# A fused four-layer cross-attention kernel: transposes of the row maxima with 128 weight columns instead of 4

## The chip, the cores and the metric

The kernel runs on one core of one Trainium2 chip. The metric is the device time of one execution in microseconds (us), median of the runs shown; lower is better. Five engines matter: TensorE (PE, with its weight loads as PEld), VectorE (DVE), ScalarE (ACT), GpSimd (POOL) and the DMA queue that SyncE feeds (SPq).

## The reference

The input `x` (4 batches, 1024 tokens, 256 channels) goes through four cross-attention layers over the same context `ctx_2048` (4 batches, 154 keys, 512 channels). Layers 0 and 2 are wide (16 heads of 64), with a bias on the logits of chosen keys; layers 1 and 3 are narrow (16 query heads of 16 on 4 key heads) with an RMS norm ahead.

```python
# wide (L0, L2)
q = (x @ Wq) ; k = (ctx @ Wk) ; v = (ctx @ Wv)             # 16 heads of 64
logits = einsum('bhqd,bhkd->bhqk', q, k) * 64 ** -0.5
logits = logits + col_bias                                  # -20 * (1 - mask) on 4 chosen keys
x = einsum('bhqk,bhkd->bhqd', softmax(logits), v) @ Wo + bo + x
# narrow (L1, L3)
xn = x * rsqrt(mean(x * x) + 1e-5) * norm_w
scores = einsum('btgrd,bsgd->bgrts', xn @ wq, ctx @ wk) / 16 ** 0.5
x = x + einsum('bgrts,bsgd->btgrd', softmax(scores), ctx @ wv) @ wo
```

The softmax subtracts the maximum of each row of logits over the 154 keys; the kernel finds these maxima first and folds them, with a minus sign, into the score matmuls.

## The kernel before, in words

`prepare` makes the keys, the values and split weights (the first 190 us). `layers` then runs two layers at a time over 4 batches and 2 pairs of layers, in halves of 512 tokens. Its work is cut into steps: 16 to a batch, each of four heads on one half of the tokens, 128 in all. A step has these parts:

- "query": six fp32r matmuls of 512 columns each (L1470) make the queries of two heads or of a group; ACT copies them (L1225, L1226), and DVE rounds and subtracts (L1377 to L1380). Only then can "max" of that step start.
- "max", eight per step: a rough bf16 product of 128 tokens with the 154 keys of two heads (L1485 wide, L1489 narrow) in a PSUM bank of `general`, which DVE reduces to two maxima per token (L1390), so that `tops` gets 4 maxima for each of 4 blocks of 128 tokens.
- "turn": four transposes (L1496) bring these maxima from columns into rows. The block of `tops` is the weight operand and the identity `ident_bf` (128 columns) streams past it; ACT copies the 4 rows, negated, into rows of `q_aux` (L1248).
- "rest" and "score": the real products (L1513, L1516, L1524, L1525) and ACT's exponentials (L1238); "value": products with the values and the sums (L1540 with 64 weight columns, L1544, L1550 and L1554 with 32; in narrow steps L1560 and L1566 with 32). "sums", "inverse", "scale", "norm", "low" and "output" (L1584, six matmuls for each of two banks) finish a chunk.

All engines walk one hand-written list (`FIRST`, `ORDER`, `LAST`, joined in `PLAN`), so every engine issues its share of the parts in that order and waits by semaphores. The part "turn n" stands in it mostly behind the query of a later step and ahead of a "value", a "rest" or a "max". Of the 128 turns, counted along PE's order of instructions, the neighbours are:

| before the turn | after the turn | turns |
|---|---|---|
| 128 weight columns | 128 weight columns | 64 |
| 128 weight columns | 64 weight columns (L1540) | 47 |
| 64 weight columns (L1540) | 64 weight columns (L1540) | 9 |
| 128 weight columns | 32 weight columns (L1560) | 5 |
| 64 weight columns | 128 weight columns | 2 |
| 32 weight columns | 128 weight columns | 1 |

Of the 67 turns with 128 weight columns behind them, 47 have an fp32 or fp32r matmul there (23 L1524, 20 L1470, 4 others) and 20 a bf16 one (19 L1489, 1 L1485).

The rows of zeros and constants that several tiles need are cleared by DVE and POOL when `layers` starts; SyncE waits for six of DVE's memsets (`rows_cleared`, L1179) before it goes on issuing loads.

Of the kernel before, what the change touches and what calls it, by code (L numbers as in the profile page):

```python
# [16 lines left out]
BF16 = mybir.dt.bfloat16  # L17
# [5 lines left out]
P = 128  # L23
# [477 lines left out]
def first_tile(n):  # L501

    return 12 * (n // 8) + (2 * (n % 8) if wide(n) else 4 + n % 8)
# [318 lines left out]
def layers(nc, ins, dr, out):  # L822

    ctx = ExitStack()
    with ctx:
        def sb(name, shape, dt=F32):
            return ctx.enter_context(nc.sbuf_tensor(name, shape, dt))
# [17 lines left out]
        w_aux, n_aux = (sb(a + "_aux", [P, H, P], BF16) for a in "wn")  # L845
        w_top, n_top = (sb(a + "_top", [P, H, KEYS], BF16) for a in "wn")
        w_rest, w_aux_rest = sb("w_rest", [P, H, 32]), sb("w_aux_rest", [P, H, 32], BF16)
        n_pair_rest, n_aux_rest = sb("n_pair_rest", [P, KVN, P], F32R), sb("n_aux_rest", [P, KVN, P], BF16)
# [5 lines left out]
        q_aux = sb("q_aux", [P, 2, 2, 4, TOK], BF16)  # L854
# [4 lines left out]
        spread_sums, inv = sb("spread_sums", [P, TOK // 8]), sb("inv", [P, TOK // 8])  # L859
        inv_b, inv_n = sb("inv_b", [P, 2, TOK]), sb("inv_n", [P, 2, TOK])  # L860
        a_hi, a_lo = sb("a_hi", [P, 2, TOK], F32R), sb("a_lo", [P, 2, TOK], F32R)
        tops = sb("tops", [P, 2, 4, 4], BF16)
        meansq, rate, power = sb("meansq", [P, 4]), sb("rate", [P, 4]), sb("power", [P, 4])
        ident, ident_bf, ones = sb("ident", [P, P]), sb("ident_bf", [P, P], BF16), sb("ones", [P, 1])
        sel, sel_rest = sb("sel", [P, 4, 32]), sb("sel_rest", [P, 4, 32])
# [3 lines left out]
        out_ps = ctx.enter_context(nc.psum_tensor("out_ps", [P, 2, 512], F32))  # L869
        sum_ps = ctx.enter_context(nc.psum_tensor("sum_ps", [P, 512], F32))  # L870

        ROWS_CLEARED, CLEARED = 6, 9


        WIDE_QUERY, KEY_ROWS, WIDE_OUT = 16 * 2, 16 * 8, 16 * 2
# [479 lines left out]

        @block.vector
        def _(dve):
            for buf in (w_top, q_aux, w_aux, w_aux_rest, n_aux, n_aux_rest):
                nc.vector.memset(buf[:].bitcast(F32), 0.0).then_inc(rows_cleared, 1)
            for buf in (n_top, n_val_rest, sel, sel_rest):  # L1360
                nc.vector.memset(buf[:].bitcast(F32), 0.0).then_inc(cleared, 1)
# [3 lines left out]
            for g in range(4):  # L1365
                nc.vector.memset(sel[:, g, 8 * g:8 * g + 8], 1.0)
                for j in range(4):
                    last = nc.vector.memset(sel_rest[32 * j:32 * j + REST, g, 8 * g:8 * g + 8], 1.0)
# [73 lines left out]
        def _(pe):  # L1442
# [3 lines left out]
            def bank(use):  # L1446

                if USE[use] >= GB:
                    w, what, n, k, m = GENERAL[USE[use] - GB]
                    read = reader[what]  # L1450
                    wait(pe, read.sem, read.after(w, what, n, k) - (read.times - 1 - m if what == "output" else 0))
                return general[:, USE[use] % GB, :]

            def do(it, what, n, k):
                if what == "query":
# [9 lines left out]
                    ps = bank((it, what, n, k, 0))  # L1465
# [3 lines left out]
                    for i, (l, r) in enumerate(pairs):  # L1469
                        last = nc.tensor.matmul(ps, l, r, start=(i == 0), stop=(i == len(pairs) - 1))  # L1470
                    last.then_inc(pe_query.sem, 1)
                elif what == "max":
# [7 lines left out]
                    ps = bank((it, what, n, k, 0))  # L1480
                    sub, pair = slice(k % 4 * P, k % 4 * P + P), k // 4
                    q = q_aux[:, half_of(n), slot(n)]
                    if wide(n):
                        for i in range(2):
                            last = nc.tensor.matmul(ps[:, i * KEYS:(i + 1) * KEYS], q[:, 2 * pair + i, sub],  # L1485
                                                    w_top[:, 4 * (n % 4) + 2 * pair + i, :], start=True, stop=True)
                    else:
                        h = 4 * (n % 4) + 2 * pair
                        last = nc.tensor.matmul(ps[:, 0:2 * KEYS], q[:, n % 2, sub],  # L1489
                                                n_top[:, h:h + 2, :].rearrange("p h k -> p (h k)"), start=True, stop=True)  # L1490
                    last.then_inc(pe_max.sem, 1)
                elif what == "turn":
                    wait(pe, dve_max.sem, dve_max.after(it, "max", n, 7))
                    ps = bank((it, what, n, k, 0))
                    for sub in range(4):
                        last = nc.tensor.transpose(ps[0:4].bitcast(BF16)[:, sub * P:(sub + 1) * P], tops[:, n % 2, sub, :], ident_bf[:])  # L1496
                    last.then_inc(pe_turn.sem, 1)
                elif what in ("rest", "score"):
                    number = pe_score.after(it, what, n, k)
                    ps = score_ps[:, number % 2, :]  # L1500
# [10 lines left out]
                    if what == "rest" and wide(n):  # L1511
# [3 lines left out]
                        for j in range(4):  # L1515
                            last = nc.tensor.matmul(ps[32 * j:32 * j + 32], w_aux_rest[:, 4 * g + j], q_aux[:, t, s, j, :],  # L1516
                                                    start=False, stop=True, skip_group_check=True)
                    else:
# [6 lines left out]
                        last = nc.tensor.matmul(ps, keys[1], q_aux[:, t, s, unit, :], start=False, stop=True)  # L1525
                    last.then_inc(pe_score.sem, 1)
                elif what == "value":
# [9 lines left out]
                    if wide(n):  # L1537
                        for i in range(2):
                            h = 4 * g + 2 * k + i
                            last = nc.tensor.matmul(out_ps[64 * i:64 * i + 64, k, :], w_val[:, h * DW:(h + 1) * DW], probs[:, 2 * k + i, :],  # L1540
                                                    start=True, stop=False, skip_group_check=True)
                        if k == 1:
# [9 lines left out]
                            for j in range(4):  # L1552
                                rows = slice(32 * j, 32 * j + REST)
                                last = nc.tensor.matmul(sum_ps[SUMS[j]], sel_rest[rows, g, :], rest[rows],  # L1554
                                                        start=False, stop=(g == 3), skip_group_check=True)
                    else:
                        out = out_ps[:, tile % 2, :]
                        for j in range(4):
                            at = 32 * block_of(n, j)
                            last = nc.tensor.matmul(out[at:at + 32], n_val[:, g, :], probs[:, j, :],  # L1560
                                                    start=True, stop=False, skip_group_check=True)
                        if n % 2:
                            for step in (n - 1, n):
                                for j in range(4):
                                    rows, at = slice(32 * j, 32 * j + REST), 32 * block_of(step, j)
                                    last = nc.tensor.matmul(out_ps[at:at + 32, first_tile(step) % 2, :], n_val_rest[rows, step % 4, :],  # L1566
                                                            probs_rest[rows, step % 4, :], start=False, stop=True, skip_group_check=True)
                    last.then_inc(pe_value.sem, 1)
                elif what == "output":
# [8 lines left out]
                    for m in range(KC):  # L1578
                        ps = bank((it, what, n, k, m))
# [3 lines left out]
                        for i, (l, r) in enumerate(pairs):  # L1583
                            last = nc.tensor.matmul(ps, l, r, start=(i == 0), stop=(i == len(pairs) - 1))  # L1584
                        last.then_inc(pe_output.sem, 1)
                elif what == "give":
# [5 lines left out]
                    ps = bank((it, what, n, k, 0))  # L1592
                    of = fetch_to[:, i % 2] if n < 6 else x[:, n % 2]
                    for t in range(2):
                        for c in range(KC):
                            at = (2 * k + t) * P
                            last = nc.tensor.transpose(ps[:, t * C + c * P:t * C + c * P + P], of[:, c, at:at + P], ident[:])
                    last.then_inc(pe_give.sem, 1)
                elif what == "square":
                    wait(pe, act_square.sem, act_square.after(it, "squares", n, k))  # L1600
                    ps = bank((it, what, n, k, 0))
                    for sub in range(4):
                        for c in range(KC):
                            last = nc.tensor.matmul(ps[:, sub:sub + 1], xn[:, c, sub * P:(sub + 1) * P], ones[:],
                                                    start=(c == 0), stop=(c == KC - 1))
                    last.then_inc(pe_square.sem, 1)
                elif what == "rate":
                    wait(pe, pool_rate.sem, pool_rate.after(it, "square", n, k))
                    ps = bank((it, what, n, k, 0))
                    for sub in range(4):  # L1610
                        last = nc.tensor.transpose(ps[:, sub * P:(sub + 1) * P], rate[:, sub:sub + 1].to_broadcast([P, P]), ident[:])
                    last.then_inc(pe_rate.sem, 1)

            def query_for(n, k):

                return ("query", n, k) if wide(n) else ("query", n - n % 2, 0)

            each_batch(pe, do)


# [5 lines left out]
def store_outputs(nc, dr, out):  # L1626

    layers(nc, dr["ins"], dr, out)
# [32 lines left out]
```

## Time and profile before

| | |
|---|---|
| median of 3 runs | 1791.41 us (1787.99 to 1791.44) |
| the profiled execution's own time | 1801.82 us |
| its span, first to last instruction | 1800.0 us |
| mean granted TensorE clock | 0.963 of 2.4 GHz |
| PE busy | 1655.3 us (92%), 10732 matmuls |
| DVE busy | 1221.1 us (68%) |
| ACT busy | 1024.6 us (57%) |
| POOL busy | 462.0 us (26%) |

PE's busy time counts the modelled tail of each matmul, so matmuls that are issued back to back overlap in it; how fast PE goes is read from the distance between two starts in the timeline. A row of the timeline that holds several matmuls (x4) gives the start of the first and the time until the end of the last.

### The profile page before, as it was taken

To read this page: it belongs to the slowest core of one execution; us is meant where nothing else is said; L and a number is where in the kernel's file an instruction comes from. 1 tells how busy PE (TensorE), PEld (TensorE's weight loads), DVE (VectorE), ACT (ScalarE), POOL (GpSimd) and SP (SyncE) were. 2 spreads that over 40 slices of the span, in tenths; PEclk is the share of its full clock that TensorE was granted. 3 is DMA by queue.
4 is the path that set the end of the run, shared out by engine and by line. 5 is a ranking of instruction groups with operands and counts; after the bars stand their busy time and mean duration, and the time that the engine had idled before them with its cause. 6 is when DMAs were issued, how large, how long until landed. Compare 5 with 4: busy or idle time off the path is not lost.

```text
span 1800.0 us, 29688 instructions
## 1 busy us (share of the span) xinstructions
PE 1655.3 (92%) x10732; PEld 894.5 (50%) x10732; DVE 1221.1 (68%) x2339; ACT 1024.6 (57%) x1737; POOL 462.0 (26%) x325
## 2 busy tenths in 40 slices
PE   6999568999999999999999999999999999999884
PEld 5787334444544445454545454545444545444442
DVE  4474536676868786777766777677777877786551
ACT  2120146576666676667666766576666766666442
POOL 4242301122222232213231313122322222232212
PEclk9998689999999999999999999999999999999987
DMA  8996621050215121513244222413251225031422
GB/s 279 326 315 207 178 80 38 27 103 25 75 38 116 33 72 29 127 24 82 66 106 105 62 62 78 88 40 71 47 111 26 80 40 121 26 78 23 119 67 79
DMA packets 177459, 165.30 MB, mean 92 GB/s; under 512 B 91802, under 2 KB 133146, under 8 KB 175778
## 3 DMA queue, kind: packets, MB, share of 16 engines
q1 hardware_dynamic: 175010, 152.91, 33.2%
q10 hardware_dynamic: 2304, 10.49, 1.5%
q8 instruction: 87, 1.43, 0.3%
q14 instruction: 58, 0.48, 0.1%
HBM read 117.73 MB, written 45.58 MB: 91 GB/s over the span
## 4 chain that ended last, share of the span: by engine, by line
PE 48%; issue 12%; DVE 11%; SPq 6%; POOL 5%; ACT 3%; DMA 3%; POOLq 0%; ACTq 0%; DVEq 0%
PE general L1584 9%; PE general L1470 8%; PE score_ps L1524 6%; PE score_ps L1525 5%; PE out_ps L1540 4%; POOL kept L1346 4%; PE general L1489 3%; PE general L1485 3%; SPq L1022 3%; DVE q_aux L1378 2%; PE score_ps L1513 2%; PE out_ps L1560 2%; DVE q_pair L1379 2%; DVE q_pair L1380 2%; DVE q_aux L1377 2%
## 5 line engine op out<-in xcount | busy, mean ns | idle before, releaser
L1390 DVE TENSOR_REDUCE tops<-general 128x2 bf16<-128x308 f32 x1024 | 434.9, 471 | 125.7 <-PE general L1485 75.2
L1238 ACT ACTIVATE probs<-score_ps 128x512 f32<-128x512 f32 x512 | 299.1, 598 | 171.8 <-PE score_ps L1525 160.0
L1346 POOL TENSOR_TENSOR kept<-kept,inv_b 128x512 f32<-128x512 f32 x128 | 169.0, 1341 | 470.7 <-DMA inv_b<-scratch_inverses 458.5
L1377 DVE CAST q_aux<-q_pair 64x512 bf16<-64x512 f32 x160 | 89.1, 557 | 194.9 <-ACT q_pair L1226 193.6
L1248 ACT ACTIVATE q_aux<-general 4x512 bf16<-4x512 bf16 x320 | 187.2, 585 | 40.2 <-PE general L1496 34.5
L1225 ACT ACTIVATE q_pair<-general 64x512 fp32r<-64x512 f32 x160 | 94.5, 591 | 128.7 <-PE general L1470 127.4
L1334 POOL TENSOR_TENSOR x_lo<-xn,x_hi 128x1024 fp32r<-128x1024 f32 x32 | 75.8, 2370 | 322.6 <-ACT x_hi L1206 188.8
L1485 PE MATMUL general<-w_top,q_aux 128*128 128x154 bf16 x1024 | 131.9, 235 | 26.8 <-DVE q_pair L1380 17.2
L1403 DVE TENSOR_TENSOR a_lo<-kept,a_hi 128x512 fp32r<-128x512 f32 x160 | 121.4, 791 | 44.8 <-ACT a_hi L1285 44.0
L1423 DVE TENSOR_TENSOR x<-general,x 128x512 f32<-128x512 f32 x160 | 106.9, 689 | 62.9 <-PE general L1584 61.8
L1285 ACT ACTIVATE a_hi<-kept 128x512 fp32r<-128x512 f32 x160 | 93.5, 625 | 97.6 <-PE general L1584 43.1
L1260 ACT ACTIVATE kept<-out_ps 128x512 f32<-128x512 f32 x192 | 104.2, 595 | 70.6 <-PE sum_ps L1554 55.2
L1489 PE MATMUL general<-n_top,q_aux 128*128 128x308 bf16 x512 | 126.4, 302 | 17.4 <-DVE q_pair L1380 13.3
L1485 PEld LDWEIGHTS general<-w_top,q_aux 128*128 128x128 bf16 x1024 | 79.8, 99 | 119.4 <-issue 56.6
L1524 PE MATMUL score_ps<-q_pair,w_pair 128*128 128x512 f32 x256 | 124.4, 490 | 14.4 <-ACT probs_rest L1238 14.2
L1540 PE MATMUL out_ps<-probs,w_val 128*64 128x512 f32 x512 | 135.7, 615 | 0.0
L1524 PE MATMUL score_ps<-q_pair,n_pair 128*128 128x512 f32 x256 | 126.4, 505 | 4.4 <-ACT probs L1238 4.4
L1346 POOL TENSOR_TENSOR kept<-kept,inv_n 128x512 f32<-128x512 f32 x64 | 82.4, 1308 | 185.9 <-DMA inv_n<-scratch_inverses 185.9
L1470 PE MATMUL general<-x_hi,wq_hi 128*128 128x512 f32 x256 | 114.7, 448 | 13.9 <-POOL x_lo L1334 12.5
L1584 PE MATMUL general<-a_hi,wo_hi 128*128 128x512 f32 x256 | 112.3, 439 | 5.6 <-DVE q_pair L1380 2.8
L1379 DVE TENSOR_TENSOR q_pair<-general,q_pair 64x512 fp32r<-64x512 f32 x160 | 109.5, 684 | 5.0
L1380 DVE TENSOR_TENSOR q_pair<-general,q_pair 64x512 fp32r<-64x512 f32 x160 | 111.0, 694 | 2.2
(149 smaller groups left out, 3238.7 us busy)
## 6 DMA issues: line engine op xcount, KB each, us to landing
inv_b<-scratch_inverses SPq DMA_DIRECT2D x128, 256.0 KB, 4.8
xn<-scratch_stream SPq DMA_DIRECT2D x16, 512.0 KB, 3.4
w_pair<-scratch_wk_hi SPq DMA_DIRECT2D x32, 256.0 KB
x<-scratch_stream SPq DMA_DIRECT2D x16, 512.0 KB, 3.3
inv_n<-scratch_inverses SPq DMA_DIRECT2D x256, 32.0 KB, 1.8
scratch_stream<-x SPq DMA_DIRECT2D x14, 512.0 KB, 4.8
scratch_wk_hi<-p_kout_hi SPq DMA_DIRECT2D x16, 308.0 KB
p_raw<-in_L_xattn_Wk_dram SPq DMA_DIRECT2D x4, 1024.0 KB, 7.9
```

What stands on the lines that cost most here:

```text
L1238: nc.scalar.activation(dst, score_ps[:, number % 2, :], ACT.Exp, scale=scale).then_inc(act_exp.sem, 1)
L1248: last = nc.scalar.activation(q_aux[a:a + 4, half_of(n), slot(n), j, :], ps[0:4].bitcast(BF16)[:, 0:TOK], ACT.Copy, scale=-1.0)
L1346: last = nc.gpsimd.tensor_tensor(tiles[i], tiles[i], (inv_b, inv_n)[n % 2][:, i, :], ALU.mult)
L1379: nc.vector.tensor_tensor(q_pair[64:P, s, j, :], ps[0:64], q_pair[0:64, s, j, :], ALU.subtract)
L1380: last = nc.vector.tensor_tensor(q_pair[0:64, s, j + 1, :], ps[64:P], q_pair[64:P, s, j + 1, :], ALU.subtract)
L1390: last = nc.vector.tensor_reduce(tops[:, n % 2, sub, 2 * pair:2 * pair + 2], src, AX_X, ALU.max)
L1470: last = nc.tensor.matmul(ps, l, r, start=(i == 0), stop=(i == len(pairs) - 1))
L1485: last = nc.tensor.matmul(ps[:, i * KEYS:(i + 1) * KEYS], q[:, 2 * pair + i, sub], w_top[:, 4 * (n % 4) + 2 * pair + i, :], start=True, st ...
L1489: last = nc.tensor.matmul(ps[:, 0:2 * KEYS], q[:, n % 2, sub], n_top[:, h:h + 2, :].rearrange("p h k -> p (h k)"), start=True, stop=True)
L1524: nc.tensor.matmul(ps, keys[0], q_pair[:, s, unit, :], start=True, stop=False)
L1540: last = nc.tensor.matmul(out_ps[64 * i:64 * i + 64, k, :], w_val[:, h * DW:(h + 1) * DW], probs[:, 2 * k + i, :], start=True, stop=False, ...
L1584: last = nc.tensor.matmul(ps, l, r, start=(i == 0), stop=(i == len(pairs) - 1))
```

## The change

`tops` gets 128 columns for each block of 128 tokens instead of 4. DVE clears it once at the start; the maxima are still written to columns 0 to 3, and the other 124 stay zero. The four transposes of a turn now take the whole block as weights and write 128 rows of the bank instead of 4; ACT still reads rows 0 to 3. The count of memsets that `rows_cleared` stands for goes from 6 to 7.

```diff
-        tops = sb("tops", [P, 2, 4, 4], BF16)
+        tops = sb("tops", [P, 2, 4, P], BF16)
...
-        ROWS_CLEARED, CLEARED = 6, 9
+        ROWS_CLEARED, CLEARED = 7, 9
...
-            for buf in (w_top, q_aux, w_aux, w_aux_rest, n_aux, n_aux_rest):
+            for buf in (w_top, q_aux, w_aux, w_aux_rest, n_aux, n_aux_rest, tops):
                 nc.vector.memset(buf[:].bitcast(F32), 0.0).then_inc(rows_cleared, 1)
...
                     for sub in range(4):
-                        last = nc.tensor.transpose(ps[0:4].bitcast(BF16)[:, sub * P:(sub + 1) * P], tops[:, n % 2, sub, :], ident_bf[:])
+                        last = nc.tensor.transpose(ps.bitcast(BF16)[:, sub * P:(sub + 1) * P], tops[:, n % 2, sub, :], ident_bf[:])
```

No instruction changes its place. On PE a turn behind the output of a narrow layer and ahead of a score stands so (the shape is rows written by columns streamed):

```order
 L1584 MATMUL general<-a_hi,no_lo 128x512
-L1496 MATMUL general<-ident_bf,tops 4x128 x4
+L1496 MATMUL general<-ident_bf,tops 128x128 x4
 L1524 MATMUL score_ps<-q_pair,n_pair 128x512
 L1525 MATMUL score_ps<-q_aux,n_aux 128x512
```

The four transposes keep their place and their 128 streamed columns; only the number of weight columns, and so of rows written, is another. All 128 turns change in this way. On DVE, where `layers` starts, one memset comes in:

```order
 L1359 MEMSET n_aux 128x1024
 L1359 MEMSET n_aux_rest 128x256
+L1359 MEMSET tops 128x512
 L1361 MEMSET n_top 128x1232
 L1361 MEMSET n_val_rest 128x128
```

The memset is the last of those that SyncE waits for. ACT, POOL and SyncE keep every instruction.

## Rows read from the trace of the kernel before

**Rows 1.** The page: busy time of three engines, their share of the span, instructions

```profile
PE 1655.3 (92%) x10732; PEld 894.5 (50%) x10732; DVE 1221.1 (68%) x2339; ACT 1024.6 (57%) x1737; POOL 462.0 (26%) x325
```

**Rows 2.** Busy time by stretch (us): PE, PEld, DVE, ACT, POOL, clock, DMA

```profile
850.00:1050.00 200.00, 195.48 (x1322) 99.80 (x1320) 150.13 (x286) 133.36 (x231) 54.38 (x38) 1.00 0.37 89
1450.00:1650.00 200.00, 191.22 (x1304) 95.99 (x1302) 148.34 (x276) 130.16 (x225) 51.75 (x38) 0.99 0.29 63
```

**Rows 3.** What PE waited for: us in total, times, longest us

```profile
PE general L1485 <- DVE q_pair L1380: 17.2, 23, 2.3
PE score_ps L1524 <- ACT probs_rest L1238: 14.2, 1, 14.2
```

**Rows 4.** PE's timeline, 762.4 to 764.0: a turn between fp32r matmuls, 128 weight columns

```profile
762.90 0.40 PE L1470 MATMUL general<-x_hi,wq_lo 128*128 128x512 f32 x1
763.22 0.39 PE L1496 MATMUL general<-ident_bf,tops 128*4 128x128 bf16 x4
763.54 0.50 PE L1470 MATMUL general<-x_hi,wq_hi 128*128 128x512 f32 x1
763.88 0.40 PE L1470 MATMUL general<-x_lo,wq_hi 128*128 128x512 f32 x1
```

**Rows 5.** Groups by line: the turn's matmul and weight load; the wide max's

```profile
L1496 PE MATMUL general<-ident_bf,tops 128*4 128x128 bf16 x512 | 50.3, 222 | 3.5 <-DVE q_pair L1380 3.4
L1496 PEld LDWEIGHTS general<-ident_bf,tops 128*4 128x4 bf16 x512 | 26.1, 84 | 52.9 <-issue 43.2 <-DVE tops L1390 9.2
L1485 PEld LDWEIGHTS general<-w_top,q_aux 128*128 128x128 bf16 x1024 | 79.8, 99 | 119.4 <-issue 56.6 <-DVE tops L1390 12.3 <-DVE q_aux L1378 7.6
```

**Rows 6.** PE's timeline, 784.6 to 785.5: bf16 between fp32r, all 128 weight columns

```profile
784.82 0.40 PE L1584 MATMUL general<-a_hi,wo_lo 128*128 128x512 f32 x1
785.06 0.31 PE L1485 MATMUL general<-w_top,q_aux 128*128 128x154 bf16 x2
785.17 0.48 PE L1470 MATMUL general<-x_hi,wq_hi 128*128 128x512 f32 x1
785.49 0.40 PE L1470 MATMUL general<-x_lo,wq_hi 128*128 128x512 f32 x1
```

**Rows 7.** PE's timeline: short bf16 and fp32 matmuls with 128 weight columns

```profile
805.70 0.58 PE L1485 MATMUL general<-w_top,q_aux 128*128 128x154 bf16 x6
...
794.08 1.88 PE L1604 MATMUL general<-ones,xn 128*128 128x1 f32 x16
```

**Rows 8.** PE's timeline, 775.9 to 776.2: from 128 to 64 weight columns

```profile
775.86 0.30 PE L1485 MATMUL general<-w_top,q_aux 128*128 128x154 bf16 x2
776.09 1.08 PE L1540 MATMUL out_ps<-probs,w_val 128*64 128x512 f32 x4
```

**Rows 9.** PE's timeline, 834.2 to 835.0: a turn between bf16 matmuls

```profile
834.42 0.29 PE L1489 MATMUL general<-n_top,q_aux 128*128 128x308 bf16 x1
834.64 0.39 PE L1496 MATMUL general<-ident_bf,tops 128*4 128x128 bf16 x4
834.96 0.31 PE L1489 MATMUL general<-n_top,q_aux 128*128 128x308 bf16 x1
```

**Rows 10.** PE's timeline, 852.2 to 852.3: a turn ahead of 32 weight columns

```profile
852.24 0.22 PE L1496 MATMUL general<-ident_bf,tops 128*4 128x128 bf16 x1
852.26 0.62 PE L1560 MATMUL out_ps<-probs,n_val 128*32 128x512 f32 x1
```

**Rows 11.** Timelines of DVE and of SyncE's queue where `layers` starts

```profile
197.49 0.91 DVE L1359 MEMSET w_aux<- 128x1024 f32 x1 [0.16 <-issue]
198.40 0.27 DVE L1359 MEMSET w_aux_rest<- 128x256 f32 x1
...
200.05 1.32 SPq L1058 DMA_DIRECT2D q_aux<-scratch_maskrows  x4
```

**Rows 12.** PE's timeline: a turn and the wait of the max behind it

```profile
799.60 0.39 PE L1496 MATMUL general<-ident_bf,tops 128*4 128x128 bf16 x4
...
804.26 0.29 PE L1485 MATMUL general<-w_top,q_aux 128*128 128x154 bf16 x2 [0.65 <-DVE q_pair L1380]
```

## The prediction

> **What bounds the kernel now.** I read the page first. PE is busy for 92% of the span, DVE for 68%, ACT for 57% [rows 1]. The stretches say where the rest of the span lies: in the steady part, about 230 to 1650 us, PE is busy for 191 to 195 of every 200 us, at a granted clock of 0.99 to 1.00, and DVE for about 150 [rows 2]. So PE sets the pace there, and a nanosecond that PE no longer spends between two matmuls is mostly a nanosecond of the kernel. The table of waits says where it is not: PE waits now and then for the queries of the step to come, the chain from the query matmul over ACT and DVE to the first max, 23 times for 17.2 us on the wide max alone, and once for 14.2 us near 262 us, where `layers` is still being loaded [rows 3].
>
> The busy shares can't show what this change touches, because modelled tails of matmuls overlap the next ones. The timeline does, by the distance between starts.
>
> **The turn as it is.** Take the turn at 763.22 [rows 4]. The fp32r matmul before it starts at 762.90, the turn 0.32 us later. The four transposes take 0.39 us to the end of the last and one takes 0.222 [rows 5], so they start (0.39 - 0.222)/3 = 0.056 us apart, and the last starts at 763.39. The next fp32r matmul starts at 763.54, 0.15 later, and the one after it at 763.88: 0.49 from the last transpose to the second fp32r matmul.
>
> Now the same without a turn, where the bf16 matmul has 128 weight columns [rows 6]. From fp32r at 784.82 to bf16 at 785.06 it is 0.24, not 0.32. The second bf16 matmul starts 0.067 later (its spacing comes from a row of six, which takes 0.58 where two take 0.31, [rows 6, 7]), at 785.13, and from there to the second fp32r matmul, at 785.49, it is 0.36, not 0.49. The fp32r matmul that begins early, 0.04 behind the bf16 one, then holds its successor for 0.32, so only the sum over two matmuls may be compared.
>
> What separates the two cases is the number of weight columns. That it is this number and not the transposing is seen where no turn is near [rows 8]: two bf16 matmuls with 128 columns start at 775.86 and 775.93, and the next one, with 64 columns, at 776.09, which is 0.16 and so 0.09 more than the spacing of 0.067. A step from one number of columns to another thus costs PE about 0.09 us, and a turn of 4 columns between matmuls of 128 makes two such steps.
>
> **The Trainium skill** has this as a rule too ("TensorEngine Tiling (Array Packing)", Key Properties: a change of the tiling mode drains the engine), and it prices no such drain; the 0.09 us above is this trace's. The same skill has a rule that speaks against the change; it is weighed with the rivals.
>
> **The change part by part.** I count the places over all 128 turns, with the table of neighbours.
>
> 1. Way in. 116 turns stand behind a matmul with 128 columns. In 111 of them (64 + 47) the step on the way in goes: 0.32 becomes 0.24, and behind a bf16 matmul 0.22 becomes 0.13 [rows 4, 6, 9]: at 834.42 the max of 308 columns starts, whose streaming takes 308/2.4 = 0.128 us at the full clock, and the turn comes 0.22 later. I take 0.09: 111 x 0.09 = 10.0 us.
> 2. Way out to fp32 or fp32r, 128 columns: 47 turns, one of which waits anyway. 0.49 becomes 0.36, or less by 0.01 since a transpose streams 128 columns and not 154; I take 0.13: 46 x 0.13 = 6.0 us.
> 3. Way out to bf16, 128 columns: 20 turns. In [rows 9] the last transpose starts at 834.64 + 0.17 = 834.81 and the max at 834.96, 0.15 later, where 0.056 would do: 20 x 0.094 = 1.9 us.
> 4. Way out to 64 columns, 47 turns, and the 9 turns between L1540 and L1540: the number of columns changes as before (128 to 64 where it was 4 to 64, [rows 8]). Nothing.
> 5. The 5 turns ahead of L1560. Here 4 columns and 32 columns run side by side: L1560 starts 0.02 behind the first transpose [rows 10]. With 128 columns this ends and a step of 0.09 comes in, while the one on the way in goes. The four transposes streamed through the same columns as the first L1560 anyway, so I take nothing; at worst it is the whole turn, 5 x 0.22 = 1.1 us.
> 6. The four transposes themselves. They stream 128 columns as before. Their weight load is of 128 x 128 instead of 128 x 4. It must keep under 0.056 us of spacing to cost nothing. The nearest row is the wide max: bf16, 128 x 128 weights, spacing 0.069 for 154 columns, which is 154/2.4 = 0.064 of streaming alone [rows 7]. So such a load doesn't take more than about 0.067. Bounds: 0 to 512 x 0.011 = 5.6 us. I take 0, since the load of 128 x 128 lasts 99 ns in its own row against 84 ns of 128 x 4 [rows 5], a difference of 15 ns that is hidden in the same way.
> 7. The memset of `tops`, 128 x 512: between 0.27 us for 256 and 0.91 for 1024 [rows 11], so about 0.48 us. SyncE's queue begins at 200.05, when the last of the six memsets ends, and then issues without a pause up to the loads that PE's long waits of that stretch end on. All of it is on the path: +0.5 us.
> 8. DVE's reduces write two values to a block as before, ACT reads the same four rows: nothing.
>
> On PE: 10.0 + 6.0 + 1.9 = 17.9 us, 1.0% of the span.
>
> **What arrives at the end.** Time saved inside a chain on which PE then waits is lost again. Of those waits the frequent one comes 4.7 us behind a turn (as at 804.26, after the turn at 799.60 [rows 12]): the query has already left PE when the turn comes, so the wait simply grows by what the turn gave. About 30 of the 128 turns lie in such a place, with the first and the last few, where loads and the final output set the pace: about a quarter. Three quarters of 17.9 is 13.4, less 0.5 for the memset: **12.9 us faster**. Nothing new becomes late by it: DVE, the next engine, keeps 50 us of every 200 idle [rows 2], and the chains that feed PE start earlier by the same amount.
>
> Against the profiled execution (1801.82 us, span 1800.0) this gives 1788.9. That execution took 10.4 us more than the median of 1791.41; the working is of differences, so from the median: **1778.5 us**.
>
> **The rivals.**
>
> - *The waits take most of it.* PE also waits in small ways: the weight loads of L1485 wait 12.3 us for DVE to reduce its banks [rows 5]. If DVE in truth paces the stretches of maxima, most turns give their time back there. A third of 17.9 would remain: 6.0 - 0.5, so 1786. For it: DVE is at 75% in the steady part. Against: PE at 96 to 98% [rows 2].
> - *The change does not do what it seems.* The step might belong to something a turn keeps, as its write of bf16 into PSUM or the change from fp32r. Then only the memset is left: 1792. Against it are [rows 6, 8], with a change from fp32r without a step and a step without a turn.
> - *Slower: the weight load comes onto the path.* The fp32 matmuls of one streamed column [rows 7] start 1.88/16 = 0.118 us apart at most: there the load of 128 x 128 sets the pace, since nothing streams. If the bf16 load of a turn took as long, spacing would go from 0.056 to about 0.109. That is 512 x 0.053 = 27.1 us more on PE, against 17.9 less; added time at the bound is kept whole, and with the memset it is +10, so 1801. It decides from a spacing of 0.056 + 17.9/512 = 0.091 on. Against it: the wide max's 0.069 [rows 7]. The nearest in doubt is that the max loads while 154 columns stream and a turn while 128 do.
>
> The Trainium skill has the rule behind this last rival ("TensorE: Matmul & The Clock Gate", LDWEIGHTS: a load takes the number of its columns over 1.2 GHz, whatever its rows), by which 4 columns are an estimated 3 ns and 128 are 107 ns. By it the time would be that of the rival. The same page (Weight-path perf modes) lets a load of exactly 128 columns that aren't fp32 run faster; this trace agrees with the second, by the 0.069 us of the wide max.
>
> **How the numbers follow.** Forecast as above, from half to all of what PE saves arriving and the load costing up to 3 us: 0.64, from 1772 to 1785. Waits take most: 0.14. No effect: 0.10. Slower: 0.12. The range leaves out the slower rival and little else: 1771 to 1793. About 0.2% (3.6 us) is what a measurement of this kernel can tell from no change: faster takes the forecast and nearly all of the first rival, 0.77; within 0.2%, the rest of it and the second, 0.11; slower 0.12.
>
> **What would show it.** In the profile of the changed kernel: the turn starts 0.24 behind an fp32r matmul; its four transposes still take about 0.39; from the last of them to the second fp32r matmul 0.35; 0.15 to L1540 as before; PE's waits for `q_pair` longer by 0.1 to 0.2 us each. A turn of 0.5 us or more would mean the load is on the path, and a way in of 0.32 that the number of columns isn't the cause.

## The result

| | before | changed |
|---|---|---|
| median | 1790.97 us (20 runs, 1782.87 to 1797.63) | 1784.25 us (20 runs, 1777.00 to 1793.44) |
| ratio | | 0.9968, 95% interval 0.9954 to 0.9981 |
| profiled execution: own time, span | 1801.82, 1800.0 us | 1788.92, 1787.1 us |

The change is faster by 0.32%, 5.7 us (3.4 to 8.2); the two medians lie 6.7 us apart. The forecast was 12.9 us. A repetition beside later experiments gave 0.9964 (0.9949 to 0.9979). The two profiled executions lie 12.9 us apart, which looks like the forecast met; it isn't, as the last section shows.

The turn of [rows 4], between fp32r matmuls with 128 weight columns, in PE's timeline of the changed kernel:

```profile
761.90 0.40 PE L1470 MATMUL general<-x_hi,wq_lo 128*128 128x512 f32 x1
762.14 0.40 PE L1496 MATMUL general<-ident_bf,tops 128*128 128x128 bf16 x4
762.35 0.47 PE L1470 MATMUL general<-x_hi,wq_hi 128*128 128x512 f32 x1
762.66 0.40 PE L1470 MATMUL general<-x_lo,wq_hi 128*128 128x512 f32 x1
```

It starts 0.24 us behind the fp32r matmul, where it was 0.32. From the start of the matmul ahead to the start of the second fp32r matmul behind it is 0.76 us, where it was 0.98. The groups by line say what the transposes cost, against [rows 5]:

```profile
L1496 PE MATMUL general<-ident_bf,tops 128*128 128x128 bf16 x512 | 51.6, 224 | 4.8 <-DVE q_pair L1380 3.4 <-DVE tops L1390 1.4
L1496 PEld LDWEIGHTS general<-ident_bf,tops 128*128 128x128 bf16 x512 | 31.3, 99 | 42.9 <-issue 34.2 <-DVE tops L1390 6.2
```

The weight load lasts 99 ns instead of 84, as that of the wide max does, and four transposes end 0.40 us after the first began instead of 0.39: a spacing of (0.40 - 0.224)/3 = 0.059 instead of 0.056. The load is hidden but for 3 to 4 ns at each of the three spacings, about 12 ns a turn behind an fp32r matmul and 2 ns behind a bf16 one (medians of all such turns).

A turn between bf16 matmuls, as in [rows 9], and one ahead of a max behind a narrow output:

```profile
835.36 0.29 PE L1489 MATMUL general<-n_top,q_aux 128*128 128x308 bf16 x1
835.49 0.39 PE L1496 MATMUL general<-ident_bf,tops 128*128 128x128 bf16 x4
835.72 0.29 PE L1489 MATMUL general<-n_top,q_aux 128*128 128x308 bf16 x1
...
829.51 0.40 PE L1496 MATMUL general<-ident_bf,tops 128*128 128x128 bf16 x4
829.95 0.29 PE L1489 MATMUL general<-n_top,q_aux 128*128 128x308 bf16 x1
```

The first pair of maxima is 0.36 us apart instead of 0.54. In the second place the max starts 0.44 behind the first transpose, where 0.23 would do (835.49 to 835.72). In the 6 turns of this kind the max starts 0.67 behind the last L1584 before and after the change (medians), although the turn comes 0.09 earlier: PE is there early and waits.

And the pair of [rows 12], a turn ahead of L1540 and the wait for DVE behind it:

```profile
799.97 0.40 PE L1470 MATMUL general<-x_hi,wq_lo 128*128 128x512 f32 x1
800.21 0.40 PE L1496 MATMUL general<-ident_bf,tops 128*128 128x128 bf16 x4
800.54 1.08 PE L1540 MATMUL out_ps<-probs,w_val 128*64 128x512 f32 x4
801.55 1.07 PE L1544 MATMUL sum_ps<-probs,sel 128*32 128x512 f32 x8
...
804.97 0.30 PE L1485 MATMUL general<-w_top,q_aux 128*128 128x154 bf16 x2 [0.73 <-DVE q_pair L1380]
```

The way out to 64 columns is 0.33 from the first transpose, 0.15 from the last, as before. The wait was 0.65 us and is 0.73: longer by 0.08, which is what this turn gave. This is one wait; the whole kernel is another matter, see below.

Over the 128 turns, the medians of each kind of neighbour give what PE saves: 47 ahead of L1540 save 0.076 us each (3.6 us), 28 between fp32r and fp32r or fp32 of 128 columns 0.22 (6.1), the others with 128 columns on both sides, but for 6, 0.20 to 0.23 (about 4.5); the 6 behind L1584 and ahead of L1489 save nothing, as above, and the 5 ahead of L1560 cost 0.06 each. That is about 14 us.

### The profile page after: what moved, and what is told of

The parts are those of the page before. It is cut to its first block, busy times and chain, and to the rows that moved or that the text cites. A ratio compares the mean times of both kernels' runs of the same rounds, so it can differ in the third digit from the quotient of the medians.

```text
span 1787.1 us, 29689 instructions
## 1 busy us (share of the span) xinstructions
PE 1641.3 (92%) x10732; PEld 898.4 (50%) x10732; DVE 1223.1 (68%) x2340; ACT 1025.5 (57%) x1737; POOL 463.3 (26%) x325
## 4 chain that ended last, share of the span: by engine, by line
PE 49%; issue 12%; DVE 11%; SPq 6%; POOL 5%; ACT 4%; DMA 3%; POOLq 0%; ACTq 0%; DVEq 0%
PE general L1584 9%; PE general L1470 8%; PE score_ps L1524 6%; PE score_ps L1525 5%; PE out_ps L1540 4%; POOL kept L1346 4%; PE general L1485 3%; PE general L1489 3%; SPq L1022 3%; PE out_ps L1560 2%; PE score_ps L1513 2%; DVE q_aux L1378 2%; DVE q_pair L1379 2%; DVE q_pair L1380 2%; DVE q_aux L1377 2%
## 5 line engine op out<-in xcount | busy, mean ns | idle before, releaser
L1377 DVE CAST q_aux<-q_pair 64x512 bf16<-64x512 f32 x160 | 82.7, 517 | 192.4 <-ACT q_pair L1226 191.6
L1403 DVE TENSOR_TENSOR a_lo<-kept,a_hi 128x512 fp32r<-128x512 f32 x160 | 126.7, 824 | 41.1 <-ACT a_hi L1285 40.2
L1489 PE MATMUL general<-n_top,q_aux 128*128 128x308 bf16 x512 | 127.1, 303 | 17.7 <-DVE q_pair L1380 13.0
L1524 PE MATMUL score_ps<-q_pair,w_pair 128*128 128x512 f32 x256 | 126.1, 498 | 12.7 <-ACT probs_rest L1238 12.5
L1540 PE MATMUL out_ps<-probs,w_val 128*64 128x512 f32 x512 | 135.8, 616 | 0.0
L1470 PE MATMUL general<-x_hi,wq_hi 128*128 128x512 f32 x256 | 113.8, 445 | 14.8 <-POOL x_lo L1334 12.5
L1584 PE MATMUL general<-a_hi,wo_hi 128*128 128x512 f32 x256 | 109.9, 429 | 5.9 <-DVE a_lo L1403 2.5
L1379 DVE TENSOR_TENSOR q_pair<-general,q_pair 64x512 fp32r<-64x512 f32 x160 | 109.5, 684 | 5.0
L1380 DVE TENSOR_TENSOR q_pair<-general,q_pair 64x512 fp32r<-64x512 f32 x160 | 111.0, 694 | 2.2
```

Of the source, the lines that this page charges most:

```text
L1379: nc.vector.tensor_tensor(q_pair[64:P, s, j, :], ps[0:64], q_pair[0:64, s, j, :], ALU.subtract)
L1380: last = nc.vector.tensor_tensor(q_pair[0:64, s, j + 1, :], ps[64:P], q_pair[64:P, s, j + 1, :], ALU.subtract)
L1524: nc.tensor.matmul(ps, keys[0], q_pair[:, s, unit, :], start=True, stop=False)
```

## The experiments

Two theories stood first. **A**: PE saves those 14 us, but only about 0.4 of it arrives, because PE's waits for DVE grow. **B**: three quarters arrive, and something that comes with the wide tile (the memset, the wider write or the clock) costs the rest back.

### Which number of columns makes the step

e1: `tops` and the transposes 32 columns wide. e2: 64.

```diff
-        tops = sb("tops", [P, 2, 4, P], BF16)
+        tops = sb("tops", [P, 2, 4, 32], BF16)
...
-   nc.tensor.transpose(ps.bitcast(BF16)[:, ...], tops[:, n % 2, sub, :], ident_bf[:])
+   nc.tensor.transpose(ps[0:32].bitcast(BF16)[:, ...], tops[:, n % 2, sub, :], ident_bf[:])
```

> The changed kernel with 32 instead of 128 weight columns in the turn (124 zero columns become 28). Theory A (the number of columns decides the step; PE saves about 14.5 us in the changed kernel but only about 0.4 of it arrives, since PE's waits for DVE grow): 32 columns are the same kind as 4, so a turn still starts 0.32 us behind an fp32r matmul of 128 columns and the next wide one 0.15 behind it; time as before, ratio 0.998 to 1.002. Theory B (three quarters of PE's saving arrives, and something else that the wide tile brings, such as the memset, the wider write or the clock, costs about 6 us): the same steps, and part of those 6 us without a gain, ratio about 1.002 to 1.003. If the zeros or the write and not the number of columns made the gain, the turn would start at 0.24 here.

Measured: 1.0018 (1.0004 to 1.0033). From its timeline:

```profile
801.58 0.40 PE L1470 MATMUL general<-x_hi,wq_lo 128*128 128x512 f32 x1
801.91 0.40 PE L1496 MATMUL general<-ident_bf,tops 128*32 128x128 bf16 x4
802.24 1.08 PE L1540 MATMUL out_ps<-probs,w_val 128*64 128x512 f32 x4
```

The turn starts at 0.33: with 32 columns, 28 of them zeros, the step is there as with 4. So neither zeros as such nor a write of 32 rows instead of 4 make the gain. The time is a little above before; 12 ns a turn of slower loads are 1.5 us, and the rest of the 3.2 us lies within the interval (from 0.7 us up). Between the theories e1 decides nothing: 1.0018 lies in A's range and next to B's 1.002 to 1.003, and the interval holds both.

> The changed kernel with 64 weight columns in the turn. If a step belongs to a change of the number of columns, it is now at the way in from 128 (0.32), at the way out to 128, but gone on the way out to L1540 (64 columns): 0.055 to 0.07 there and not 0.15, and both steps of the 9 turns between L1540 and L1540 are gone. PE: 47 x 0.09 + 9 x 0.19 = about 6 us less than before. Theory A: about 0.4 of that, ratio 0.998 to 1.000. Theory B: 0.997. If instead only 128 against fewer than 128 matters, the way out to L1540 stays at 0.15 and the time is that of before.

Measured: 0.9994 (0.9973 to 1.0014).

```profile
794.45 0.40 PE L1470 MATMUL general<-x_hi,wq_lo 128*128 128x512 f32 x1
794.77 0.35 PE L1496 MATMUL general<-ident_bf,tops 128*64 128x128 bf16 x3
794.91 0.64 PE L1540 MATMUL out_ps<-probs,w_val 128*64 128x512 f32 x1
794.97 0.22 PE L1496 MATMUL general<-ident_bf,tops 128*64 128x128 bf16 x1
795.02 1.02 PE L1540 MATMUL out_ps<-probs,w_val 128*64 128x512 f32 x3
795.98 1.06 PE L1544 MATMUL sum_ps<-probs,sel 128*32 128x512 f32 x8
```

The step is at the way in (0.32) and gone on the way out: L1540 even starts between the transposes. From the last L1470 to L1544 it is 1.53 us, against 1.58 in the changed kernel and 1.65 with 4 columns (the median of 33 such places). Equal numbers of columns made no step, at 128 and at 64. Unequal ones need not make one: 4 columns ahead of 32 had none in [rows 10]. The way out was expected at 0.055 to 0.07; that it would overlap was not. The ratio fits A (0.998 to 1.000), and B's 0.997 lies just outside the interval.

### How much of PE's time arrives

e3 makes the four transposes of a turn twice, e4 makes one of four (in e4 the maxima of the first 128 tokens stand for all 512, and ACT reads that block four times).

```diff
-                    for sub in range(4):
+                    for sub in (0, 1, 2, 3, 0, 1, 2, 3):     (e3)
+                    for sub in range(1):                     (e4)
```

> The changed kernel with each turn's four transposes made twice (the second four write the same values again): PE has 512 more transposes at about 0.058 us, 29.7 us more. Theory A: the waits that swallow savings also swallow part of what is added, so 0.4 to 0.6 of it, 12 to 18 us, shows; ratio to before 1.003 to 1.007. Theory B (PE sets the end nearly everywhere): 0.75 or more of it, 22 to 30 us; ratio 1.009 to 1.014.

> The changed kernel with one transpose instead of four in each turn; ACT reads that block four times, so its work stays the same. (The maxima of the first 128 tokens of a half stand for all 512: part of the computation is left out.) PE has 384 transposes less at about 0.058 us, 22 us less than the changed kernel. Theory A: 0.3 to 0.4 of it arrives, 7 to 9 us, ratio to before 0.991 to 0.993. Theory B: 0.75 of it, 17 us, ratio to before 0.986 to 0.988.

| kernel | PE's time against before | ratio to before | time against before | share that arrives |
|---|---|---|---|---|
| e3 | -14 + 29 = +15 us | 1.0045 (1.0024 to 1.0067) | +8 us | 0.5 |
| changed | -14 us | 0.9968 (0.9954 to 0.9981) | -5.7 us | 0.4 |
| e4 | -14 - 22 = -36 us | 0.9928 (0.9908 to 0.9948) | -13 us | 0.36 |

Both fall where A put them and outside B's. The three kernels have the same wide tile and the same memset, so what the tile costs is in all of them and drops out between them: from e4 to e3 PE has 51 us more to do and the time grows by 21, a share of 0.4. With the intervals, the shares of the table are 0.3 to 0.8, 0.2 to 0.6 and 0.3 to 0.5, so whether the share falls as more is taken away can't be told. Part of where it goes is seen in what PE waited for in e4:

```profile
PE general L1485 <- DVE q_pair L1380: 19.1, 21, 2.0
PE general L1489 <- DVE q_pair L1380: 15.3, 14, 2.0
...
PE general L1584 <- DVE q_pair L1380: 5.4, 9, 1.8
```

In the changed kernel the same three are:

```profile
PE general L1485 <- DVE q_pair L1380: 17.7, 22, 2.1
...
PE general L1489 <- DVE q_pair L1380: 13.0, 10, 2.0
...
PE general L1584 <- DVE q_pair L1380: 1.5, 3, 1.0
```

39.8 us against 32.2: of the 22 us that e4 takes off PE, these rows alone take 7.6 back. For the change itself the same rows show nothing: they sum to 33.3 us before and 32.2 in the changed kernel (28.7 in e8, the changed kernel again). All idle time of PE, span less busy time, is 144.7 us before, 145.8 in the changed kernel and 142.2 in e8; e9, with 4 columns, has 137.7 and e4 153.4. A growth of 8 us would have to be seen against differences of 4 to 7 between executions of the same kind.

The stretches in which the granted clock is 1.00 in every one of these traces show more. Summed over 800 to 1100, 1150 to 1290 and 1335 to 1480 us, with some 50 of the 128 turns, for before and e9 (4 columns), the changed kernel and e8 (128 columns), e3 and e4:

```profile
sum 585.00, PE 574.84 PEld 286.25 DVE 436.77 ACT 393.74 POOL 157.67; mean PE 191.61 PEld 95.42 DVE 145.59 ACT 131.25 POOL 52.56
sum 585.00, PE 575.13 PEld 285.97 DVE 437.00 ACT 394.04 POOL 157.39; mean PE 191.71 PEld 95.32 DVE 145.67 ACT 131.35 POOL 52.46
sum 585.00, PE 571.27 PEld 288.24 DVE 442.09 ACT 394.89 POOL 157.71; mean PE 190.42 PEld 96.08 DVE 147.36 ACT 131.63 POOL 52.57
sum 585.00, PE 571.54 PEld 289.67 DVE 444.81 ACT 392.70 POOL 159.82; mean PE 190.51 PEld 96.56 DVE 148.27 ACT 130.90 POOL 53.27
sum 585.00, PE 575.54 PEld 299.95 DVE 431.17 ACT 390.23 POOL 151.68; mean PE 191.85 PEld 99.98 DVE 143.72 ACT 130.08 POOL 50.56
sum 585.00, PE 561.94 PEld 279.47 DVE 445.19 ACT 393.66 POOL 161.20; mean PE 187.31 PEld 93.16 DVE 148.40 ACT 131.22 POOL 53.73
```

PE is idle for 10.2 and 9.9 us with 4 columns, 13.7 and 13.5 with 128, 9.5 in e3 and 23.1 in e4. The change takes an estimated 5.5 us off PE there (50/128 of 14), and 3.6 of it come back as idle time; cut at the same instructions of PE instead of at the same times, it is 2 to 4. So here the waits do take about half of the saving. How the rest of the 8 us is spread over the remaining kernel, single executions can't show.

### Taking the wait away

The wait is for a PSUM bank that the query occupies until DVE has subtracted (L1380). e5 (4 columns) and e6 (128 columns) shorten that: the low halves of the queries are made for 8 of 512 columns, so this part of the computation is left out. L1380 is cut in the same way as L1379, which is shown, and ACT waits for the clearing of `q_pair`. DVE is busy for 1048 us instead of 1221 by it, so these two runs shorten the chain and unload DVE at once.

```diff
-   nc.vector.tensor_tensor(q_pair[64:P, s, j, :], ps[0:64], q_pair[0:64, s, j, :], ALU.subtract)
+   nc.vector.tensor_tensor(q_pair[64:P, s, j, 0:8], ps[0:64, 0:8], q_pair[0:64, s, j, 0:8], ALU.subtract)
...
-            for buf in (w_top, q_aux, w_aux, w_aux_rest, n_aux, n_aux_rest):
+            for buf in (q_pair, w_top, q_aux, w_aux, w_aux_rest, n_aux, n_aux_rest):
```

> The kernel before (4 weight columns) with a short chain from the query to the max: L1379 and L1380 subtract 8 columns instead of 512, so DVE is rid of about 1.3 us in each of 160 queries. (The low halves of the other 504 columns stay zero: part of the computation is left out; q_pair is cleared at the start, 3.5 us, and ACT waits for the clearing.) To be read against e6. Theory A (PE's savings are swallowed by its waits for DVE behind the query): these waits, 35 us in the kernel before, shrink to under 10, and the time falls by 15 to 25 us, ratio 0.986 to 0.993. Theory B (the waits have nothing to do with it): no statement on this kernel alone.

> The same short chain in the changed kernel (128 weight columns; same parts left out). Theory A: with the waits behind the query gone, 0.7 or more of the 14.5 us that PE saves arrives: 10 us or more less than e5. Theory B (something that comes with the wide tile costs back what is missing): the difference to e5 stays at 6 us, as it was between the two kernels.

Measured: e5 0.9862 (0.9841 to 0.9883), e6 0.9810 (0.9792 to 0.9829). PE's waits for `q_pair` in e5 and in e6 (lines stand two further down here):

```profile
PE general L1487 <- DVE q_pair L1382: 2.7, 3, 1.0
PE general L1498 <- DVE q_pair L1382: 2.4, 1, 2.4
...
PE general L1491 <- DVE q_pair L1382: 0.7, 2, 0.5
```

```profile
PE general L1487 <- DVE q_pair L1382: 2.4, 3, 1.1
PE general L1498 <- DVE q_pair L1382: 2.4, 1, 2.4
...
PE general L1491 <- DVE q_pair L1382: 0.5, 2, 0.3
```

The waits of 17.2 us in [rows 3] are down to 2.7, and they don't grow with 128 columns. The same change of `tops` is now worth 1768.96 - 1759.69 = 9.3 us by the medians of 4 runs each, 0.66 of 14. A had said 10 or more and B 6; 9.3 is nearer to A, but short of its bound. The ratio of the two ratios is 0.9947, with an interval of about 0.992 to 0.997, and the 5.7 us of the full kernel lie at its edge. So the times alone point to A without excluding B. That the waits for `q_pair` are gone in both speaks for A; it doesn't tell the wait for the bank from DVE's load, which fell with it.

### Is it the memset

> The changed kernel's tile of 128 columns and its memset, but transposes of columns 0 to 3 alone: only the memset (0.48 us) is new against the kernel before. Theory A: 0.5 us, ratio 0.999 to 1.001. Theory C (the memset holds the loads up by more than its length, which is where part of the gain went; e1 with its small memset was 0.18% slower than before): 2 to 4 us, ratio 1.001 to 1.002.

```diff
-   nc.tensor.transpose(ps.bitcast(BF16)[:, ...], tops[:, n % 2, sub, :], ident_bf[:])
+   nc.tensor.transpose(ps[0:4].bitcast(BF16)[:, ...], tops[:, n % 2, sub, 0:4], ident_bf[:])
```

Measured: 1.0007 (0.9992 to 1.0023). The memset lasts 0.48 us, and this fits its length; the upper end, 4 us, isn't excluded by this run alone. Theory C's 1.001 to 1.002 lies within the interval too, so this run doesn't decide between A and C.

### A turn for each neighbour

e7 takes the number of columns from what stands behind the turn, and the memset out of SyncE's way; e12 is e7 again; e10 has the memset where the changed kernel has it; e11 has 128 columns only in the 67 turns with 128 columns behind them, and 4 elsewhere.

```diff
+def turn_columns(it, n):
+    behind = next(x for x in PLAN[PLAN.index((it, "turn", n, 0)) + 1:] if x[1] in PE_PARTS)
+    if behind[1] != "value":
+        return P
+    return 64 if wide(behind[2]) else 4
...
-   nc.tensor.transpose(ps.bitcast(BF16)[:, ...], tops[:, n % 2, sub, :], ident_bf[:])
+   nc.tensor.transpose(ps[0:turn_columns(it, n)].bitcast(BF16)[:, ...], tops[:, n % 2, sub, 0:turn_columns(it, n)], ident_bf[:])
```

> The changed kernel with the number of weight columns of each turn set by what stands behind it on PE: 64 ahead of L1540 (56 turns), 4 ahead of L1560 (5), 128 else; and the memset of tops taken from the group that SyncE waits for. By e2's profile a turn of 64 columns ahead of L1540 makes the stretch up to L1544 0.05 us shorter than 128 columns do (47 turns) and 0.25 us shorter between two L1540 (9): PE saves about 5 us more than the changed kernel. Theory A: 0.4 of it and the 0.5 us of the memset: 2 to 3 us, ratio to before 0.995 to 0.996. Theory B: 0.75 of it, ratio 0.994.

> The changed kernel as it is, beside the others. Both theories: ratio as measured, 0.995 to 0.998.

> e7 with the memset back among those that SyncE waits for. Theory A: 0.5 us slower than e7. Theory C: 2 to 4 us slower than e7.

> 128 weight columns only in the 67 turns that have a matmul of 128 columns behind them, 4 in the others; memset as in the changed kernel. These 67 turns hold about 10.5 of the 14.5 us that PE saves. Theory A: 0.4 of it arrives, 4 us, ratio 0.997 to 0.999. If it is as fast as the changed kernel (0.9964 to 0.9968) or faster, the turns ahead of L1540, which stand behind a query, brought nothing.

> e7 once more, on the chip of e9 to e11. Both theories: ratio 0.991 to 0.995.

| kernel | ratio to before | interval |
|---|---|---|
| e7 | 0.9927 | 0.9906 to 0.9949 |
| e12, e7 again | 0.9953 | 0.9934 to 0.9973 |
| e10, memset back | 0.9963 | 0.9942 to 0.9984 |
| e8, the changed kernel again | 0.9964 | 0.9949 to 0.9979 |
| e11, 67 turns alone | 0.9977 | 0.9961 to 0.9993 |

e7's median was better than both theories had it, though its interval holds B's 0.994, and its repetition, 0.9953 where 0.991 to 0.995 was expected, says that part of this was luck: together about 0.994, 11 us faster than before. Beside each other, e7 beats the changed kernel (e8) by 0.37%, more than 5 us on PE can explain at a share of 0.4; the intervals touch, and how much of it is real stays open. e11 fits A: 4 us of 10.5, with an interval of 1 to 7. It can't be told from the changed kernel, so it doesn't show what the turns ahead of L1540 are worth. Between e10 and e12 lie 0.1%, which tells neither 0.5 us nor 2 us from nothing. What the memset costs at the end is bounded by e9 and not measured.

## Why the prediction was wrong

The forecast was 12.9 us; 5.7 were measured, almost the 5.5 of the first rival. That the figures meet is partly luck: this rival had two thirds of 17.9 go in small waits in the stretches of maxima, but PE saves 14, and its waits for DVE's reduces (`tops`) sum to 5.2 us before and 7.1 in the changed kernel, 1.9 more and not 12. Step by step:

- **PE sets the pace in the steady part.** Too strong. Behind PE's busy share of 96% stand waits that end on DVE's time, and they are longer when PE comes earlier (10 us of 585 against 13.6, above).
- **Way in and way out.** Right in size: 0.09 in (0.32 to 0.24), 0.13 out to fp32r (0.98 to 0.76 over both), 0.09 out to bf16, nothing ahead of 64 columns.
- **The transposes.** Taken as free, with 0.011 us each as the bound; it is 0.003 to 0.004, up to 12 ns a turn, 1.5 us together at most. The slower rival (a spacing of 0.109) is thereby ruled out. By the Trainium skill ("TensorE: Matmul & The Clock Gate", LDWEIGHTS) a load of 128 columns takes an estimated 107 ns; this trace has 59 ns from one transpose to the next, so no such time lies between these bf16 transposes.
- **PE's sum, 17.9 us.** About 14. Besides the loads, the 6 turns ahead of L1489 gave nothing, for the max waits there for DVE anyway, and the 5 ahead of L1560 cost 0.3.
- **The memset.** 0.48 us in the profile, as predicted. That all of it lies on the path isn't shown: SyncE's queue begins at 200.05 us in both profiled executions, since DVE began its memsets 0.53 us earlier in the changed one.
- **What arrives: three quarters.** This step failed. It counted the waits that stood in the list behind a turn and held every other turn's saving for kept. e3 and e4 give a share of 0.36 to 0.5, and between e5 and e6, where the wait for the query's bank is short, it is about two thirds. The mechanism named (the wait at 804.26 grows by what the turn at 799.60 gave) was right at that place, and its reach was not. The likely reason is that a saving that is kept at the next wait is lost at a later one, where PE comes earlier to a bank that DVE frees on its own time: in the stretches at full clock PE's idle time grows by 3.6 of some 5.5 us saved. No run follows one turn's saving to the wait that takes it. Waits that PE did not have before appear too, as at 829.95.
- **Nothing new becomes late: DVE keeps 50 us of 200 idle.** Wrong in the same way. DVE isn't full, but its work on one query lies in a chain, and PE waits for the end of that chain (L1380). e5 and e6, which shorten it, take DVE's share down with it, so the two aren't separated.
- **The range of the forecast.** "From half to all" with a load of up to 3 us doesn't give 1772 to 1785: by the prediction's own terms it is 17.9 - 0.5 = 17.4 us at most and 9.0 - 0.5 - 3 = 5.5 at least, so 1774 to 1786.

The sum that would have held is 14 x 0.4 = 5.6; the 0.4 is taken from the runs and was not in any row before them.

That the change isn't what it seems, the second rival, is excluded by e1 and e2: the number of columns alone makes or removes the step. Nor does the clock cost the rest: the mean granted clock was 0.9652 in the 33 runs of the kernel before beside e9 and 0.9644 in the 20 of the changed kernel, and among those 33 a clock lower by 0.001 went with about 1.3 us, so this difference is worth an estimated 1 us.

Left open: whether a turn ahead of the queries, where its saving would come before the chain starts, keeps more; this wasn't tried.

## What to carry to other kernels

A change between 128, 64 and at most 32 weight columns from one matmul to the next cost about 0.09 us here, so it can pay to give a small matmul the number of what stands next to it: padding four transposes of 4 columns to 128 costs 12 ns and saves up to 0.22 in all; to 64 it costs some 26 ns (their starts span 0.192 us instead of 0.166 behind an fp32r matmul). Before a saving on the busiest engine is booked, add and remove a known amount of its work and look at the end: the share that arrives was 0.4 at 92% busy. The busy time alone doesn't say it, and neither does the list of waits of one execution.

## What the runs showed of the hardware that was not expected

**Matmuls with 64 columns overlap transposes with 64 columns.** In e2 the first L1540 starts 0.14 us after the first of the four transposes and ahead of the last (0.05 us ahead as the median of 46 such places), where 128 columns put it 0.33 behind the first.

**Stretches at half the clock fall elsewhere in each execution, and so a pair of profiles misleads.** The kernel before, in its profiled execution, ran a stretch at half the clock where the changed kernel ran less of it. Before, windows 1120 to 1139, 1139 to 1146 and 1146 to 1160 us (the columns as in [rows 2]):

```profile
1120.00:1139.00 19.00, 15.69 (x86) 9.08 (x87) 11.57 (x23) 9.36 (x17) 2.51 (x2) 1.00 0.80 145
1139.00:1146.00 7.00, 6.29 (x31) 3.75 (x28) 5.14 (x9) 4.63 (x9) 0.00 (x0) 0.52 0.82 180
1146.00:1160.00 14.00, 14.00 (x104) 6.80 (x102) 8.28 (x16) 8.64 (x15) 5.26 (x4) 1.00 0.23 50
```

The changed kernel from 1139 to 1146 us, then e8, the same kernel in another execution:

```profile
1139.00:1146.00 7.00, 6.96 (x48) 2.91 (x40) 5.06 (x10) 5.04 (x9) 0.00 (x0) 0.77 0.86 183
```

```profile
1139.00:1146.00 7.00, 7.00 (x59) 2.88 (x58) 4.68 (x10) 5.61 (x10) 1.50 (x2) 1.00 0.37 82
```

The granted clock is a mean over the window of 1.2 and 2.4 GHz: 0.52 is nearly all of it at 1.2. Ahead of it PE had waited 2.59 us for ACT:

```profile
1138.00 1.07 PE L1560 MATMUL out_ps<-probs,n_val 128*32 128x512 f32 x8 [2.59 <-ACT probs L1238]
```

But it goes the other way elsewhere: the changed kernel has such stretches near 466 and 562 us, where the one before has none, and e8 has one near 1114. Before and changed, 464 to 478, then e8, 1110 to 1122:

```profile
464.00:478.00 14.00, 11.71 (x68) 6.54 (x61) 12.21 (x19) 8.68 (x16) 4.46 (x4) 1.00 0.39 96
```

```profile
464.00:478.00 14.00, 12.47 (x63) 7.65 (x63) 10.78 (x19) 7.48 (x14) 2.93 (x3) 0.88 0.38 108
```

```profile
1110.00:1122.00 12.00, 9.79 (x47) 6.11 (x45) 8.88 (x17) 5.98 (x11) 0.59 (x1) 0.86 0.58 140
```

Compared at the same instruction of PE, the changed kernel is not ahead of the one before at 1136 us (0.4 us behind). By 1146 it has gained 1.9 us, around 1313 it gains about 4 and around 1593 some 3.5, in places where the one before has stretches at half the clock and the changed one has less or none, and 4.5 between 1700 and 1750; at the end it is 12.7. Over the whole execution the mean granted clock is the same, 0.963 and 0.964, so the clock says where the lead of this pair arose rather than why it is 12.9 us while the medians of 20 runs are 6.7 apart. The runs of the changed kernel alone spread from 1777.0 to 1793.4 us. Whether a change is worth what one pair of profiles says can't be read from their spans.
